# Four graph layers on one core: dealing out VectorE's side work anew, and normalising the last graph by halves

## The chip, the cores and the metric

The kernel runs on 1 core of one Trainium2 chip. The metric is the device time of one execution in microseconds. The kernel computes eight independent graphs, one after the other, in one launch. Its engines are TensorE (PE), VectorE (DVE), ScalarE (ACT), GpSimd (POOL) and SyncE (SP, which issues the plain loads, the transposing transfers and the stores).

## The reference

Input x is 8 x 1024 x 128 (float32), adj is 8 x 1024 x 1024 (0 or 1, about 16 ones in a row). Each graph passes four layers, and each layer adds its result to x and normalises the rows:

```
x = layernorm(x + relu([x, pool(x)] W + b))      # layer 0: pool = max over the first 25 neighbours
x = layernorm(x + elu(gat1(x, adj)))             # layer 1: softmax over neighbours, leaky relu scores
x = layernorm(x + elu(gat2(x, adj)))             # layer 2: the same form, other weights
x = layernorm(x + tanh(A tanh(A x W0 + b0) W1 + b1))   # layer 3: A = softmax(x Watt x' / sqrt(128) + mask)
layernorm(x) = (x - mean) / sqrt(var + 1e-5)     # over the 128 features
```

The maximum in layer 0 is taken over the neighbours with the 25 lowest indices of each node. It depends on the inputs alone, so a kernel may prepare it for a later graph.

## The kernel before, in words

The 1024 nodes of a graph lie in eight tiles of 128. While graph b passes its layers, the pooling of graph b+1 is prepared beside it, by two ways whose results are combined by a maximum.

**Gathered neighbours.** DVE finds a list of neighbour rows for two tiles at a time (a pair): `find_keys` (L1228 and its neighbours, "keys"), then `split_keys`, `sort_members` and `list_rows` ("members a", "b", "c"). POOL then gathers the rows from memory (`gather`, L551 to L571): 18 transfers for each of tiles 0 to 3 and 16 for each of tiles 4 to 7, each followed by a short memset. The gathered rows of a tile lie in one of three buffers (a ring, RING = 3), so tile t waits in `gather` for the pooling of tile t-3, and tile 4 for that of tile 1. DVE reduces a tile by `pool_tile` (L1327 and L1328, "pool"), and that waits until all its transfers have landed. Each engine works through its instructions in the order in which they are written, so whatever stands behind such a wait on DVE waits too.

**Picked neighbours.** The neighbours beyond the gathered ones are selected by products: for pick q, ACT or DVE makes a 0/1 matrix (`make_hot`: L632 and L635 on ACT, L1375 on DVE; MADE_BY says who makes which half), PE multiplies it with x (L903), and DVE folds the product into the running maximum (`max_pick`, L1385 and L1387). There are 16 picks for each graph after the first (26 for the first, done before graph 0 begins). PE writes pick q only when `max_pick` has read the pick before it from the same bank: pick 14 waits for `max_pick` 13 (`spare_maxed(b + 1, 13)`).

**Where side work stands.** The table SIDE names the places in DVE's program of graph b at which side work for graphs b+1 and b+2 is done; FIRST_WORK does the same for the picks ahead of graph 0. The table before has keys of (b+1, pair 1) at the head of layer 0, pooling of tile 4 behind the attention tiles ("steps"), of tile 6 between `make_hot` 12 and `max_pick` 12 ("last step"), and of tile 7 behind the last addition to x ("end").

**The end of a graph on the other engines.** PE computes the second attention product (L1150) in eight tiles, with pick 13 after the second and pick 14 after the sixth; then it packs the adjacency bits of a pair of graph b+2 (`feed`, L850), does pick 15, counts neighbours for graph b+2 (L878 to L883) and turns the next graph's x (L946). ACT converts adjacency tiles (L586), makes `hot` 14, applies tanh (L774), reads the packed bits (`take_fed`, L643), takes the counts (L613), normalises its half of the nodes (L669) and takes the turned x (L660, then L724). SP turns the packed bits by a transposing transfer for DVE's `find_keys`.

**The norm.** `layer_norm` aggregates the moments of eight tiles (L1398), computes the reciprocal root by ten small instructions on 128x8 (L1401 to L1418), and normalises tiles 0 to 3 itself (L1422); ACT normalises tiles 4 to 7 (L669) once the last of the ten is done. In the two gat layers of the last graph, which has no picks beside it, PE finishes the heads of nodes 0 to 511 first, and DVE adds each half as it comes (`take_heads`, `add_heads`).

Of the kernel before, what the change touches and what calls it, by code (L numbers as in the profile page):

```python
# [13 lines left out]
I32 = mybir.dt.int32  # L14
# [48 lines left out]
class Steps:  # L63
# [8 lines left out]
    def link(self, instruction):  # L72
# [30 lines left out]
              20: [("pool", 0, 5)],  # L103
              24: [("pool", 0, 6)],
# [3 lines left out]
SIDE = {"layer 0": [("keys", 1, 1)],  # L108
        "gat 1": [("members", 1, 1)],
# [8 lines left out]
        "steps": [("pool", 1, 4), ("keys", 2, 0), ("members", 2, 0), ("pool", 1, 5)],  # L118
        "last step": [("pool", 1, 6)],
        "end": [("pool", 1, 7)]}  # L120
# [44 lines left out]
def build_graph_layers(nc, x, adj, w0, b0, w1, b1, a1, w2, a2, watt, w3a, b3a, w3b, b3b, out):  # L165
# [13 lines left out]
    with ExitStack() as ctx:  # L179
# [398 lines left out]
        def _(act):  # L578
# [142 lines left out]
            def graph(b, slot, in_loop):  # L721
# [44 lines left out]
                feed(b, slot, 3, in_loop)  # L766
                if exists(b, 1, B, in_loop):
                    make_hot(b + 1, 14)
# [8 lines left out]
                take_fed(b, 3, in_loop)  # L777
# [49 lines left out]
        def _(pe):  # L827
# [208 lines left out]
            def graph(b, slot, in_loop):  # L1036
# [175 lines left out]
        def _(dve):  # L1212
# [181 lines left out]
            def layer_norm(slot):  # L1394

                settle()
                for t in range(T):
                    done(nc.vector.bn_aggr(moments[:, t, :], stats[:, t, :]))  # L1398
                settle()

                link(nc.vector.tensor_scalar(spread[:, :], moments[:, :, 1], EPS, None, ALU.add))  # L1401

                link(nc.vector.tensor_scalar(rstd[:, :].bitcast(I32), spread[:, :].bitcast(I32), -0.5, RSQRT_GUESS,
                                             ALU.mult, ALU.add))
                link(nc.vector.tensor_tensor(error[:, :], rstd[:, :], rstd[:, :], ALU.mult))
                link(nc.vector.scalar_tensor_tensor(out=error[:, :], in0=error[:, :], scalar=-0.5,
                                                    in1=spread[:, :], op0=ALU.mult, op1=ALU.mult))
                link(nc.vector.scalar_tensor_tensor(out=rstd[:, :], in0=error[:, :], scalar=1.5,
                                                    in1=rstd[:, :], op0=ALU.add, op1=ALU.mult))

                link(nc.vector.tensor_tensor(error[:, :], rstd[:, :], rstd[:, :], ALU.mult))
                link(nc.vector.scalar_tensor_tensor(out=error[:, :], in0=error[:, :], scalar=-THIRD,
                                                    in1=spread[:, :], op0=ALU.mult, op1=ALU.mult))
                link(nc.vector.scalar_tensor_tensor(out=error[:, :], in0=error[:, :], scalar=THIRD * 10 / 3,
                                                    in1=error[:, :], op0=ALU.add, op1=ALU.mult))
                link(nc.vector.scalar_tensor_tensor(out=rstd[:, :], in0=error[:, :], scalar=1.875,
                                                    in1=rstd[:, :], op0=ALU.add, op1=ALU.mult))
                norm_scale.raised_by(nc.vector.scalar_tensor_tensor(  # L1418
                    out=offset[:, :], in0=moments[:, :, 0], scalar=-1.0, in1=rstd[:, :],
                    op0=ALU.mult, op1=ALU.mult))  # L1420
# [3 lines left out]
                x_normed.raised_by(last)  # L1424

            def gat(b, slot, layer, in_loop):
# [70 lines left out]
                else:  # L1497
                    for h in range(2):
                        take_heads(h)
                        add_heads(h)  # L1500
                layer_norm(slot)

            def graph(b, slot, in_loop):
                flat = xs[slot][:, :, :].rearrange("p t c -> p (t c)")
                side_work(b, slot, "layer 0", in_loop)
# [6 lines left out]
                for h in range(2):  # L1512
# [51 lines left out]
                layer_norm(slot)  # L1564
# [82 lines left out]
```

How the kernel before makes its waits and increments, by code:

```python
            def load_adj(b, t, freed=None, count=None):  # L417
                source = adj_tiles[b, t]
                if freed is not None:
                    sp.wait_ge(freed.sem, count)
                    sp.sem_inc(loads_begun, 1)
                adj_loaded[t % 2].raised_by(sp.dma_start(adj_in[:, t % 2, :], source))
# [1 line left out]
            def turn(b, slot, t):  # L424
                sp.wait_ge(adj_converted.sem, adj_converted.at(b, t + 1))
                sp.sem_inc(loads_begun, 1)
                adj_t_ready[t % 2].raised_by(sp.dma_start_transpose(adj_t[slot][:, :, t * P:(t + 1) * P],
                                                                    adj_bf[:, t % 2, :]))
# [1 line left out]
            def turn_packed(b, pair):  # L430
                sp.wait_ge(packed_taken.sem, packed_taken.at(b, pair + 1))
                if not (isinstance(b, int) and b == 1 and pair == 0):
                    sp.sem_inc(loads_begun, 1)
                    sp.wait_ge(packed_read.sem, packed_read.at(b, pair))
                sp.sem_inc(loads_begun, 1)
                packed_turned.raised_by(sp.dma_start_transpose(
                    packed_t[:, :, :, :].rearrange("p h i g -> p (h i) g"),
                    group_bits[:, :, :].rearrange("p h n -> p (h n)")))
# [1 line left out]
            def load_next(b, t):  # L441
                if isinstance(b, int) and b == 0 and t < 4:
                    sp.wait_ge(first_read, 1)
                load_adj(b, t, adj_converted, adj_converted.at(b, t - 1))
```

## Time and profile before

| | |
|---|---|
| median of 3 runs | 1952.48 us (1941.37 to 1954.05) |
| the profiled execution, its time | 1933.09 us |
| its span in the profile | 1931.0 us |
| mean granted TensorE clock | 0.952 |
| PE busy | 1671.2 us (87%) |
| POOL busy | 1445.9 us (75%) |
| DVE busy | 1429.5 us (74%) |
| ACT busy | 1127.9 us (58%) |

All terms below come from the profiled execution. The span begins with the picks of graph 0 (to about 190 us), then graphs 0 to 6 follow in some 222 us each, and graph 7, which has nothing prepared beside it, takes the last 180 us. A row of a timeline gives the start, the duration, the engine, the line of the program and the operation; "xN" merges N like instructions that follow each other, and the bracket at its end gives the time that the engine sat idle before it, and who ended that.

### The profile page before, as it was taken

How to read it: one execution, taken by the hardware profiler on the slowest of the kernel's cores; microseconds unless marked ns; L12 is line 12 of the kernel's file. 1: busy time of each engine (PE TensorE's matmuls, PEld its weight loads, DVE VectorE, ACT ScalarE, POOL GpSimd, SP SyncE). 2: the span in 40 equal slices, each digit the busy share in tenths (PEclk: the TensorE clock that was granted, in tenths of full speed). 3: DMA queues.
4: the chain of work that ended last, by engine and by line, in shares of the span. 5: the costliest groups of instructions: out<-in, count | busy, mean ns of one | idle time of the engine just before them, and what ended most of it. 6: DMA issues, size and time to landing. Idle time of an engine off the chain costs nothing.

```text
span 1931.0 us, 29391 instructions
## 1 busy us (share of the span) xinstructions
PE 1671.2 (87%) x9767; PEld 1316.0 (68%) x9812; DVE 1429.5 (74%) x3427; ACT 1127.9 (58%) x1517; POOL 1445.9 (75%) x2135
## 2 busy tenths in 40 slices
PE   4777798999889898999989899998989898896777
PEld 2655676777759676677758677686757777595747
DVE  5874888768877789768886788768887688746531
ACT  6664755656665765656565665558556665652252
POOL 6888888888888888888788888888878887870000
PEclk9998899989999999998999999998999999997889
DMA  7231424343343333344233333435233522311010
GB/s 195 71 84 37 103 78 100 90 125 78 77 131 73 103 78 98 107 99 111 73 119 86 102 79 76 129 77 127 72 102 87 121 57 63 107 36 33 1 66 12
DMA packets 153282, 167.06 MB, mean 87 GB/s; under 512 B 102685, under 2 KB 119978, under 8 KB 153130
## 3 DMA queue, kind: packets, MB, share of 16 engines
q1 hardware_dynamic: 119594, 96.43, 18.6%
q0 software_dynamic: 33536, 68.75, 13.5%
q8 instruction: 77, 1.26, 0.3%
q14 instruction: 75, 0.61, 0.1%
HBM read 140.45 MB, written 4.19 MB: 75 GB/s over the span
## 4 chain that ended last, share of the span: by engine, by line
PE 43%; DVE 27%; ACT 9%; POOL 8%; issue 7%; DVEq 6%; DMA 1%; ACTq 0%; SPq 0%; POOLq 0%
PE spare L903 11%; PE big L1150 6%; POOL gathered L563 6%; PE big L1011 5%; DVEq L73 4%; PE big L1087 3%; PE big L935 3%; DVE probs_t L1454 3%; PE big L1109 3%; DVE pooled L1327 3%; ACT hot L632 2%; PE side L1127 2%; POOL pause L568 2%; DVE keys L1224 2%; PE big L1002 2%
## 5 line engine op out<-in xcount | busy, mean ns | idle before, releaser
L563 POOL DMA_INDIRECT gathered<-in_x_dram,rows x1048 | 1089.3, 1039 | 240.1 <-issue 158.4
L903 PE MATMUL spare<-hot,x_part 128*128 128x512 f32 x1552 | 393.4, 405 | 36.2 <-DVE hot L1375 27.3
L568 POOL MEMSET pause<- 32x256 bf16 x1048 | 349.9, 334 | 41.9
L903 PEld LDWEIGHTS spare<-hot,x_part 128*128 128x128 f32 x1552 | 291.4, 193 | 108.9 <-issue 21.2
L632 ACT ACTIVATE hot<-running,minus_count 128x2048 fp32r<-128x2048 bf16 (+1 forms) x131 | 251.1, 1916 | 131.8 <-PE spare L903 112.8
L635 ACT ACTIVATE hot<-hot,plus_one 128x2048 fp32r<-128x2048 f32 (+1 forms) x131 | 251.5, 1920 | 4.3
L1011 PEld LDWEIGHTS big<-values,probs_t 128*128 128x128 f32 x1792 | 219.8, 199 | 8.6
L1011 PE MATMUL big<-values,probs_t 128*128 128x129 f32 x1792 | 222.7, 283 | 0.4
L1327 DVE TENSOR_REDUCE pooled<-gathered 128x128 f32<-128x2048 f32 (+2 forms) x56 | 212.0, 3786 | 14.3 <-DMA gathered<-in_x_dram,rows 13.3
L1375 DVE TENSOR_SCALAR hot<-running 128x2048 fp32r<-128x2048 bf16 (+1 forms) x145 | 186.4, 1305 | 33.9 <-PE spare L903 16.4
L1454 DVE SCALAR_TENSOR_TENSOR probs_t<-side,col_gain,adj_t 128x1024 f32<-128x1024 f32 x128 | 154.6, 1276 | 27.3 <-ACT side L691 27.3
L1531 DVE TENSOR_REDUCE neg_max<-big 128x1 f32<-128x1024 f32 x64 | 78.1, 1220 | 98.8 <-PE big L1113 98.2
L903 PE MATMUL side<-hot,x_part 128*128 128x512 f32 x448 | 115.3, 402 | 28.8 <-DVE hot L1375 17.8
L613 ACT CAST running<-spare 128x512 bf16<-128x512 f32 x92 | 53.9, 586 | 140.4 <-remote 75.3
L745 ACT ACTIVATE work<-big,neg_max 128x1024 f32<-128x1024 f32 x64 | 71.4, 1116 | 98.8 <-DVE neg_max L1531 98.8
L1109 PE MATMUL big<-xt,queries 128*128 128x512 f32 x256 | 121.0, 595 | 6.5 <-ACT values L677 6.1
L1150 PEld LDWEIGHTS big<-values,probs_t 128*128 128x128 f32 x1024 | 117.6, 192 | 2.5 <-ACT values L677 0.9
L903 PEld LDWEIGHTS side<-hot,x_part 128*128 128x128 f32 x448 | 80.5, 188 | 56.0 <-issue 15.8
L1150 PE MATMUL big<-values,probs_t 128*128 128x128 f32 x1024 | 117.9, 274 | 0.7 <-ACT values L677 0.7
L1087 PE MATMUL big<-values,probs_t 128*128 128x128 f32 x1024 | 118.3, 274 | 0.0
L1087 PEld LDWEIGHTS big<-values,probs_t 128*128 128x128 f32 x1024 | 116.2, 192 | 0.0
L712 ACT ACTIVATE work<-work 128x512 f32<-128x512 f32 x32 | 20.0, 624 | 139.4 <-DVE work L1472 139.4
(203 smaller groups left out, 2629.5 us busy)
## 6 DMA issues: line engine op xcount, KB each, us to landing
adj_in<-in_adj_dram SPq DMA_DIRECT2D x128, 512.0 KB, 3.7
gathered<-in_x_dram,rows POOLq DMA_INDIRECT x1048
xs<-in_x_dram SPq DMA_DIRECT2D x8, 512.0 KB, 4.7
out_dram<-xs SPq DMA_DIRECT2D x8, 512.0 KB
adj_t<-adj_bf SPq DMA_TRANSPOSE x64
packed_t<-group_bits SPq DMA_TRANSPOSE x28, 2.8
w_sb<-in_L_gnn_W_dram SPq DMA_DIRECT2D x1, 128.0 KB
w_sb<-in_L_gnn_W_dram SPq DMA_DIRECT2D x2, 64.0 KB
```

What stands on the lines that cost most here:

```text
L563: (late_gathered if late else rows_gathered[t % RING]).raised_by(pool.indirect_dma_start(out=gathered[:, t % RING, k * C:(k + 1) * C], out ...
L568: last = nc.gpsimd.memset(pause[quarter:quarter + 32, k // (4 * PAUSED), :], 0.0)
L632: hot_apart.raised_by(nc.scalar.activation(chunk, running[:, tiles[0]:tiles[-1] + 1, :], ACT.Abs, bias=minus_count[:, s:s + 1]))
L635: hot_made.raised_by(nc.scalar.activation(chunk, chunk.bitcast(F32), ACT.Relu, scale=-1.0, bias=plus_one[:, 0:1]))
L903: last = nc.tensor.matmul(pick_bank(b, q), x_parts[part][:, m, :], hot[:, place_of(b, q, m), :], start=(m == 0 and part == 0), stop=(m == ...
L1011: last = nc.tensor.matmul(heads[:, t, 0:C + 1], probs_t[:, j, t * P:(t + 1) * P], values[:, j, :], start=False, stop=(j == T - 1), skip_gr ...
L1087: last = nc.tensor.matmul(low_t[:, t, :], probs_t[:, m, t * P:(t + 1) * P], values[:, m, 0:C], start=(m == 0), stop=(m == T - 1))
L1109: nc.tensor.matmul((low, high)[t % 2][:, half], queries[:, t * P:(t + 1) * P], xt[:, half], start=True, stop=False, skip_group_check=True)
L1150: last = nc.tensor.matmul(low_t[:, t, :], probs_t[:, m, t * P:(t + 1) * P], values[:, m, 0:C], start=(m == 0), stop=(m == T - 1))
L1327: link(nc.vector.tensor_reduce(pooled[:, t, :], rows_of[:, :, 0:n], AX.X, ALU.max))
L1375: hot_ready.raised_by(nc.vector.tensor_scalar(hot_chunk(b, q, c), running[:, tiles[0]:tiles[-1] + 1, :], float(wanted(b, q)), None, ALU.is ...
L1454: gat_probs.raised_by(nc.vector.scalar_tensor_tensor(out=probs_t[:, j, :], in0=gains, scalar=col_gain[:, j:j + 1], in1=adj_t[slot][:, j, : ...
```

## The change

In SIDE and FIRST_WORK, DVE's stages are moved. Keys of (graph b+2, pair 1) are now found near the end of graph b ("turned"), those of (1, 1) during the first graph's picks, and none at the head of layer 0. Tile 4 is pooled at attention tile 5, tile 6 in "steps" and tile 7 in "last step", which itself now stands behind `max_pick` 12 and `make_hot` 13 and ahead of `max_pick` 13. The last pick's maximum comes behind the norm. PE's packing for layer 3 moves from behind the attention product to behind its second tile, and ACT's reading of it ahead of `make_hot` 14. In the last graph, layers 0 to 2 call `layer_norm_half` for each half of the nodes as it is added, in place of one `layer_norm`.

```
@@ the tables
+              22: [("keys", 1, 1)],
...
-SIDE = {"layer 0": [("keys", 1, 1)],
-        "gat 1": [("members", 1, 1)],
+SIDE = {"gat 1": [("members", 1, 1)],
...
-        "steps": [("pool", 1, 4), ("keys", 2, 0), ("members", 2, 0), ("pool", 1, 5)],
-        "last step": [("pool", 1, 6)],
-        "end": [("pool", 1, 7)]}
+        "tile 5": [("pool", 1, 4)],
+        "steps": [("keys", 2, 0), ("members", 2, 0), ("pool", 1, 5), ("pool", 1, 6)],
+        "last step": [("pool", 1, 7)],
+        "turned": [("keys", 2, 1)]}
@@ ACT, layer 3
                 feed(b, slot, 3, in_loop)
+                take_fed(b, 3, in_loop)
                 if exists(b, 1, B, in_loop):
                     make_hot(b + 1, 14)
...
-                take_fed(b, 3, in_loop)
@@ PE, layer 3
+                    if t == 1 and exists(b, 2, B, in_loop):
+                        feed(b, slot, 3, in_loop)
                     if t in (1, 5) and exists(b, 1, B, in_loop):
...
-                    feed(b, slot, 3, in_loop)
@@ DVE, the norm
+            def layer_norm_half(slot, h):
+
+                scale_rows(slot, range(HALF * h, HALF * h + HALF))
+                if h == 0:
+                    norm_first_half(slot)
+                else:
+                    norm_scale.raised_by(offset_rows(slice(HALF, T)))
@@ DVE, a gat layer of the last graph
                         take_heads(h)
                         add_heads(h)
+                        layer_norm_half(slot, h)
+                    return
@@ DVE, layer 0
                     half_stats(slot, h)
+                    if not exists(b, 1, B, in_loop):
+                        layer_norm_half(slot, h)
@@ DVE, end of a graph
-                side_work(b, slot, "last step", in_loop)
                 if picks:
                     max_pick(b + 1, 12)
                     make_hot(b + 1, 13)
+                side_work(b, slot, "last step", in_loop)
+                if picks:
                     max_pick(b + 1, 13)
+                side_work(b, slot, "turned", in_loop)
                 for h in range(2):
                     dve.wait_ge(att_tanh.sem, att_tanh.at(b, 2 + h + 1))
...
-                side_work(b, slot, "end", in_loop)
+                layer_norm(slot)
                 if picks:
                     max_pick(b + 1, 15)
-                layer_norm(slot)
```

`scale_rows(slot, tiles)` holds the aggregation and nine of the ten small instructions, on the columns of the tiles named; `offset_rows` is the tenth, and `norm_first_half` normalises tiles 0 to 3.

## Rows read from the trace of the kernel before

**Rows 1.** The page, busy time of each engine, share of the span, instructions.

```profile
PE 1671.2 (87%) x9767; PEld 1316.0 (68%) x9812; DVE 1429.5 (74%) x3427; ACT 1127.9 (58%) x1517; POOL 1445.9 (75%) x2135
```

**Rows 2.** Who waited for whom: us in total, times, longest.

```profile
POOL gathered L563 <- DVE pooled L1328: 24.2, 5, 7.4
...
DVE pooled L1327 <- DMA gathered<-in_x_dram,rows: 13.3, 3, 7.5
```

**Rows 3.** Timeline of POOL: first gathers of tiles; one slow gather at 623.61.

```profile
408.16 0.95 POOL L563 DMA_INDIRECT gathered<-in_x_dram,rows  x1 [0.83 <-POOL pause L568]
...
623.61 1.75 POOL L563 DMA_INDIRECT gathered<-in_x_dram,rows  x1 [0.16 <-issue]
...
626.53 1.34 POOL L563 DMA_INDIRECT gathered<-in_x_dram,rows  x1 [0.83 <-POOL pause L568]
...
961.64 0.95 POOL L563 DMA_INDIRECT gathered<-in_x_dram,rows  x1 [6.26 <-DVE pooled L1328]
...
1065.98 0.95 POOL L563 DMA_INDIRECT gathered<-in_x_dram,rows  x1 [0.83 <-POOL pause L568]
```

**Rows 4.** Timeline of DVE, end of graph 1.

```profile
609.56 2.55 DVE L1375 TENSOR_SCALAR hot<-running 128x2048 fp32r<-128x2048 bf16 x2
...
622.24 0.69 DVE L1553 TENSOR_TENSOR xs<-xs,xt 128x512 f32<-128x512 f32 x1 [6.59 <-ACT xt L774]
...
632.05 3.71 DVE L1327 TENSOR_REDUCE pooled<-gathered 128x128 f32<-128x2048 f32 x1
...
636.27 0.69 DVE L1387 TENSOR_TENSOR best_t<-best_t,side 128x512 f32<-128x512 f32 x1
```

**Rows 5.** Timeline of DVE, keys at the head of graph 2 and what follows.

```profile
641.31 0.17 DVE L1241 TENSOR_SCALAR isolated<-degree 128x2 f32<-128x2 f32 x1
...
647.93 0.69 DVE L1508 TENSOR_TENSOR probs_t<-big,best_t 128x512 f32<-128x512 f32 x1 [0.42 <-PE big L1058]
```

**Rows 6.** Timeline of PE, end of graph 1: pick 14, first count, turning.

```profile
621.82 3.89 PE L903 MATMUL spare<-hot,x_part 128*128 128x512 f32 x16
...
633.86 0.38 PE L881 MATMUL side<-adj_t,count_all 128*128 128x512 bf16 x1
...
639.01 1.04 PE L946 MATMUL big<-ident,xs 128*128 128x128 f32 x8
```

**Rows 7.** Timeline of ACT, last count taken and start of graph 2.

```profile
639.21 0.59 ACT L613 CAST running<-side 128x512 bf16<-128x512 f32 x1
...
643.09 0.98 ACT L724 COPY work<-side 1x1024 f32<-1x1024 f32 x1
```

**Rows 8.** Timeline of ACT, the L724 copy of graphs 1, 6 and 7.

```profile
419.97 0.99 ACT L724 COPY work<-side 1x1024 f32<-1x1024 f32 x1
...
1529.07 0.98 ACT L724 COPY work<-side 1x1024 f32<-1x1024 f32 x1
...
1750.97 0.98 ACT L724 COPY work<-side 1x1024 f32<-1x1024 f32 x1
```

**Rows 9.** Timeline of DVE, pooling of tile 1 ends, graphs 1 and 6.

```profile
516.42 0.35 DVE L1328 TENSOR_SCALAR pooled<-pooled,connected,pool_floor 128x128 f32<-128x128 f32 x1
...
1625.42 0.35 DVE L1328 TENSOR_SCALAR pooled<-pooled,connected,pool_floor 128x128 f32<-128x128 f32 x1
```

**Rows 10.** Chain that ended last: last gather of graph 0's tile 7, issue to landing.

```profile
190.02 2.47 DMA gathered<-in_x_dram,rows
```

**Rows 11.** Timeline of DVE at graph 0's start, behind tile 7 and keys.

```profile
202.07 0.69 DVE L1508 TENSOR_TENSOR probs_t<-big,best_t 128x512 f32<-128x512 f32 x1
```

**Rows 12.** Timeline of DVE, last graph: norm of layer 0, second heads of layer 1.

```profile
1762.99 0.64 DVE L1398 BATCH_NORM_AGGREGATE moments<-stats 128x2 f32<-128x6 f32 x8
...
1765.89 0.17 DVE L1418 SCALAR_TENSOR_TENSOR offset<-moments,rstd 128x8 f32<-128x8 f32 x1
...
1799.76 0.18 DVE L1471 RECIPROCAL recip<-big 128x4 f32<-128x4 f32 x1 [3.11 <-PE big L1002]
```

**Rows 13.** Timeline of PE, last graph: turning after idle time.

```profile
1808.02 1.97 PE L946 MATMUL big<-ident,xs 128*128 128x128 f32 x8 [8.30 <-DVE xs L1422]
```

More of the change, by code:

```diff
@@ L1392, in half_stats, with scale_rows @@
                     done(nc.vector.bn_stats(stats[:, t, :], xs[slot][:, t, :]))
-            def layer_norm(slot):
+            def scale_rows(slot, tiles):
                 settle()
-                for t in range(T):
+                for t in tiles:
                     done(nc.vector.bn_aggr(moments[:, t, :], stats[:, t, :]))
                 settle()
[L1401 to L1420, printed above, removed]
@@ new lines, in scale_rows @@
+                part = slice(tiles[0], tiles[-1] + 1)
+                link(nc.vector.tensor_scalar(spread[:, part], moments[:, part, 1], EPS, None, ALU.add))
+                link(nc.vector.tensor_scalar(rstd[:, part].bitcast(I32), spread[:, part].bitcast(I32), -0.5,
+                                             RSQRT_GUESS, ALU.mult, ALU.add))
+                link(nc.vector.tensor_tensor(error[:, part], rstd[:, part], rstd[:, part], ALU.mult))
+                link(nc.vector.scalar_tensor_tensor(out=error[:, part], in0=error[:, part], scalar=-0.5,
+                                                    in1=spread[:, part], op0=ALU.mult, op1=ALU.mult))
@@ new lines, in scale_rows @@
+                link(nc.vector.scalar_tensor_tensor(out=rstd[:, part], in0=error[:, part], scalar=1.5,
+                                                    in1=rstd[:, part], op0=ALU.add, op1=ALU.mult))
+                link(nc.vector.tensor_tensor(error[:, part], rstd[:, part], rstd[:, part], ALU.mult))
+                link(nc.vector.scalar_tensor_tensor(out=error[:, part], in0=error[:, part], scalar=-THIRD,
+                                                    in1=spread[:, part], op0=ALU.mult, op1=ALU.mult))
@@ new lines, in scale_rows, with offset_rows @@
+                link(nc.vector.scalar_tensor_tensor(out=error[:, part], in0=error[:, part], scalar=THIRD * 10 / 3,
+                                                    in1=error[:, part], op0=ALU.add, op1=ALU.mult))
+                link(nc.vector.scalar_tensor_tensor(out=rstd[:, part], in0=error[:, part], scalar=1.875,
+                                                    in1=rstd[:, part], op0=ALU.add, op1=ALU.mult))
+            def offset_rows(part):
+                return nc.vector.scalar_tensor_tensor(
+                    out=offset[:, part], in0=moments[:, part, 0], scalar=-1.0, in1=rstd[:, part],
+                    op0=ALU.mult, op1=ALU.mult)
@@ L1421, in layer_norm, with norm_first_half @@
+            def norm_first_half(slot):
                 for t in range(T // 2):
@@ L1424, in layer_norm @@
                 x_normed.raised_by(last)
+            def layer_norm(slot):
+                scale_rows(slot, range(T))
+                norm_scale.raised_by(offset_rows(slice(0, T)))
+                norm_first_half(slot)
+            def layer_norm_half(slot, h):
+                scale_rows(slot, range(HALF * h, HALF * h + HALF))
+                if h == 0:
+                    norm_first_half(slot)
+                else:
+                    norm_scale.raised_by(offset_rows(slice(HALF, T)))
             def gat(b, slot, layer, in_loop):
@@ L1504, in graph @@
                 flat = xs[slot][:, :, :].rearrange("p t c -> p (t c)")
-                side_work(b, slot, "layer 0", in_loop)
                 for h in range(2):
@@ L1560, in graph @@
                             max_pick(b + 1, 14)
-                side_work(b, slot, "end", in_loop)
+                layer_norm(slot)
                 if picks:
                     max_pick(b + 1, 15)
-                layer_norm(slot)
             def pack_first():
```

## The prediction

> **What bounds the kernel now.** I read the page's busy times first: PE 1671 us and POOL 1446 us stand highest [rows 1], and neither is at its whole span, so the order of the work decides. The waits come next. DVE waited for gathered rows only three times in all, and POOL for DVE's pooling five times, 24.2 us [rows 2]. The reader should see two loops that run almost abreast: PE, DVE and ACT need (1529.07 - 419.97) / 5 = 221.8 us for a graph, by the L724 copy that I take as each graph's mark M [rows 8]; POOL needs less, since it is held up now and then. Third, POOL's tile boundaries. In graph 0 it starts the tile behind tile 7 at 408.16, in graph 1 at 626.53. In graph 3 it starts tile 4 at 961.64, released by DVE's pooling of tile 1, and is through tile 7 at 1065.98: 104.3 us for four tiles [rows 3]. A last gather landed 2.47 us after its start [rows 10]; the next tile's first gather starts some 2.1 us after it (0.95 gather, 0.3 memset, 0.83 idle), so a tile is in 0.3 us behind that start.
>
> Now DVE's side. Tile 7 is pooled at 632.05 without a wait [rows 4], 5 us after it landed (626.8). The change puts that pooling behind `make_hot` 13, which ends at 609.56 + 2.55 = 612.1. The data is not there for another 14.7 us. That is the heart of the matter.
>
> **The change, part by part.**
>
> *Tile 7.* Let L be the landing. Behind it, on DVE in order, stand: pooling 4.2 (632.05 to 636.27), `max_pick` 13, 0.7 [rows 4], so L + 4.9. Only then may PE start pick 14. Then keys, 641.31 to 647.5 = 6.2 [rows 5]: L + 11.1. Then the first half's addition and statistics, 1.6, begun at 622.24 when its tanh ended that idle time of 6.59 [rows 4] and now long ready: L + 12.8. `make_hot` 15, two chunks like the pair in [rows 4], 2.4 to 2.6: first chunk at 14.0, second at 15.3. PE meanwhile: pick 14, 3.9 [rows 6], two attention tiles 3.6, to L + 12.4. Pick 15 starts at 14.1 and ends at 18.0. From the first count to the turning is 5.15 [rows 6]; from it to ACT's last count copy 639.80 - 633.86 = 5.9 [rows 6, 7]: L + 24.0. ACT's four normalisations take 1.65 and the rest to the mark 1.14 (643.09 less the 641.95 at which its first copy of the turned x begins) [rows 7]. So the next M = L + 26.7. DVE's norm, done at L + 22, and `max_pick` 15 at L + 22.8 are hidden by ACT's counts, which is also why moving the norm ahead of `max_pick` 15 gains nothing here.
>
> *Where L falls.* POOL has been busy without a break up to 408.16, so nothing DVE does makes it earlier: L = 408.5 in graph 0, and M of graph 1 is 435.2 instead of 419.97, +15.2. From there each graph closes a loop. M to the end of pooling tile 1 is 96.8 in graph 1 and 96.7 in graph 6 (the first and last of six) [rows 8, 9]; this stretch is untouched. POOL starts tile 4 some 0.8 later, needs 104.3, landing 0.3: L = M + 202.2, while DVE stands at the pooling at 612.1 - 420.0 = M + 192.1, a wait of 10 us in every graph. The loop is 202.2 + 26.7 = 228.9, against 221.8: +7.1 a graph. After five more graphs M of graph 6 is 1579.7 (before 1529.07), +50.6. Its own end has no keys and no counts: L + 4.9 for `max_pick` 13, pick 14 and two attention tiles 7.5, tanh 1.1, addition 1.6, scale 3.1, ACT 2.8, together L + 21.0. So M of graph 7 is 1579.7 + 202.2 + 21.0 = 1802.9 against 1750.97 [rows 8], **+51.9**. The pooling does leave the end of graph 6, where it stood behind the last addition for 4.8 us, but the wait is what ends last.
>
> *Tiles 4 and 6.* They swap 4.2 us of DVE work around the same `max_pick` 11. Tile 6 lands 26 us before tile 7, at about M + 176, and is wanted at M + 177: no cost, or 1 to 2 us inside the later wait. In graph 0 it costs more, and that too only shortens the wait for 408.5.
>
> *Keys.* In graph 0 the first `pooled_t` stood behind keys at 202.07 [rows 11]; tile 7 was done 6 us before. Those 6.0 us are won and then waited away, because L of graph 0 is POOL's. In later graphs DVE is idle 0.42 behind the keys [rows 5]: nothing is won. In the first phase keys go before pooling of tile 6, which waited for its rows; at most 1 us, again behind a wait.
>
> *Packing.* On PE 1.0 us moves ahead of pick 13, behind the transposing transfers of two adjacency tiles. No row shows their landing; between 0 and 3 us of PE wait (the transfers are issued within 2 us of ACT's conversions). I take 1, by the nearest rows, the packed words' 2.8 us to landing; PE's coming stall for `max_pick` 13 covers it. ACT's `take_fed` waits for it ahead of `hot` 14, where ACT stood idle for pick 13 anyway. SP's transfer of the packed bits then comes some 18 us earlier, and SP's next wait is for the output, unchanged.
>
> *The last graph by halves.* One norm takes 1762.99 to 1766.06 up to the offset, 3.1, and 4.1 with DVE's own tiles [rows 12]. Half the columns save only the four aggregations (0.3); the small instructions cost the same on four columns as on eight, as far as the rows go (a bound from below: half, which would save 1 us more). So the first half costs 3.5 and delays the second half's addition, already ready in layer 0, and the scale then comes 3.2 later. Since PE can turn half of x ahead, I take +3.1 for layer 0. In the gat layers the idle 3.11 before the second heads [rows 12] covers 3.1 of 3.5; the turning behind the norm has four transposes left, -0.2 each. Sum **+2.7**, bounds 0 and +5.
>
> Sum: 1933.1 + 51.9 + 2.7 = 1987.7 on the profiled execution's scale, +54.6. The median of the runs is 1952.5, 19.4 above that execution; the difference carried over gives **2007 us**, +2.8%.
>
> **The rivals.** *A, PE falls to its low clock in the stalls.* After 8.30 us idle, eight transposes took 1.97, at 1.2 GHz, against 1.04 at 2.4 GHz [rows 13, 6]. PE now idles 5 to 7 us before pick 14. In my sum the slower pick 14 and attention hide behind keys and `make_hot` 15 up to 1.7 us; if the clock costs 3.9 more, 2.2 to 3.6 us stay, times six: 2020 to 2029. The Trainium skill, "TensorE: Matmul & The Clock Gate", "What's actually happening", says an idle array falls to half rate; by that rule this rival holds, and the trace agrees on the fall.
>
> *B, the gathers get faster.* Beside a `make_hot` of DVE a gather took 1.75 instead of 0.95 [rows 3]. If moved work avoided all of them, 64 gathers at 1.455 and four boundaries of 0.7 more are 96 us instead of 104.3, L = M + 193.9, the loop 220.6, below 221.8; only graph 0's shift and the halves stay, 1952.5 + 15.2 + 2.7 = 1970 on the median's scale, within 1%. Against it: the number of `hot` made per graph is unchanged. The Trainium skill, "GPSIMD Engine Reference", "Key points", has GpSimd share its SBUF interfaces with VectorE; by it the collisions move with the instructions, they don't vanish.
>
> *C, the other side: keys were on the path of every graph.* If tile 7 lands by M + 192 and each graph's head is bound by keys as in graph 0, 6.2 us go seven times, 5.5 at graph 6's end, and +2.7 remains: -46, 1906. It decides from L below 612 in graph 1; L is 626.8 [rows 3], and the idle 0.42 [rows 5] speaks against it too.
>
> *D, no wait but heads as I read them*: -6 - 5.5 - 3 + 2.7 = -12, 1941: within 1%.
>
> **How the numbers follow.** A measurement here tells about 1% from no change. Forecast 0.78, A 0.10, B 0.06, D 0.03, C 0.03. Slower 0.88, same 0.09, faster 0.03. The range takes the runs' spread (1941 to 1954) with 5 to 8.5 us a graph: 1941 + 15 + 25 + 0 = 1981, and 1954 + 15 + 50 + 5 = 2024; a little towards B makes 1976, towards A 2026.
>
> **What would show it.** DVE idle before L1327 or its like for DMA gathered, 9 to 12 us in each of graphs 1 to 6 and over 15 in graph 0; L724 copies 228 to 230 apart; POOL waiting for L1328 some 11 us a graph before tile 4; pick 14 released by `max_pick`; the last graph 2 to 3 us longer from its mark. It is wrong if `pool_tile` of tile 7 starts unwaited, or if L724 copies stay 222 apart.

## The result, and the profile after

| | before | after |
|---|---|---|
| median | 1951.01 us (1941.37 to 1954.05, 4 runs) | 1988.70 us (1978.24 to 1993.82, 4 runs) |
| profiled execution, its time | 1933.09 us | 1988.97 us |

The ratio is 1.0199, with a 95% interval of [1.0156, 1.0241]: slower, by 37.7 us. The forecast was 2007 (1976 to 2026). On the scale of the profiled executions the forecast was 1987.7, and it came out at 1988.97. The 18 us between the two forecasts are taken up behind the experiments.

The span is 1987.2 us, 56.2 more than before, and no engine's busy time has grown by as much: PE's is 28.6 us above [rows 1], that of its weight loads 12.7, and the others' differ by 7 us or less.

```profile
PE 1699.8 (86%) x9812; PEld 1328.7 (67%) x9812; DVE 1436.3 (72%) x3454; ACT 1127.0 (57%) x1517; POOL 1448.0 (73%) x2135
```

The waits after (us in total, times, longest) answer [rows 2]: both have grown. DVE waits for gathered rows 80.2 us instead of 13.3, POOL for pooling 73.5 instead of 24.2. A new wait of ACT, ahead of its copy at L753, was ended by nothing that the trace can name ("remote"); such waits are called ownerless below.

```profile
DVE pooled L1329 <- DMA gathered<-in_x_dram,rows: 80.2, 11, 12.6
...
POOL gathered L564 <- DVE pooled L1330: 73.5, 7, 13.5
...
ACT probs_t L753 <- remote: 26.8, 4, 7.8
```

The timeline of DVE after, at tile 7 in graphs 0 and 1, answers the row at 632.05 of [rows 4], which had no wait. `max_pick` 13 stands behind it.

```profile
407.24 3.58 DVE L1329 TENSOR_REDUCE pooled<-gathered 128x128 f32<-128x2048 f32 x1 [12.63 <-DMA gathered<-in_x_dram,rows]
...
636.44 3.79 DVE L1329 TENSOR_REDUCE pooled<-gathered 128x128 f32<-128x2048 f32 x1 [6.97 <-DMA gathered<-in_x_dram,rows]
640.31 0.35 DVE L1330 TENSOR_SCALAR pooled<-pooled,connected,pool_floor 128x128 f32<-128x128 f32 x1
640.75 0.69 DVE L1389 TENSOR_TENSOR best_t<-best_t,spare 128x512 f32<-128x512 f32 x1
```

The timeline of POOL after, at the gather behind tile 7 of graph 1 and at the first gather of tile 4 in graph 2, answers [rows 3]: the wait before tile 4 is 10.75 us. In graphs 1 to 6 it is 10.6 to 13.6 us, where before it was 0.8 to 7.4 (6.26 in the row of graph 3).

```profile
635.84 0.95 POOL L564 DMA_INDIRECT gathered<-in_x_dram,rows  x1 [0.83 <-POOL pause L569]
...
759.82 0.95 POOL L564 DMA_INDIRECT gathered<-in_x_dram,rows  x1 [10.75 <-DVE pooled L1330]
```

The marks after (ACT's copy, now at L725) answer [rows 8].

```profile
433.95 0.98 ACT L725 COPY work<-side 1x1024 f32<-1x1024 f32 x1
...
1581.74 0.98 ACT L725 COPY work<-side 1x1024 f32<-1x1024 f32 x1
...
1804.13 1.00 ACT L725 COPY work<-side 1x1024 f32<-1x1024 f32 x1 [0.95 <-PE side L1048]
```

A graph takes (1581.74 - 433.95) / 5 = 229.6 us. In graph 1, tile 7 landed at 636.2, M + 202.2. The page's shares of the chain that ended last, by engine, show the same turn: POOL had 8% of it before, and has 20% now.

```profile
PE 33%; POOL 20%; DVE 17%; issue 14%; ACT 10%; DVEq 3%; DMA 2%; another core or an unknown queue 1%; SPq 0%; POOLq 0%; ACTq 0%
```

PE's timeline at the end of graph 1, to be held against [rows 6], shows a delay that the forecast had made too small. The packing (L851) waits for the transposing transfer, and pick 13 stands behind it. Pick 14 comes at 643.91 without idle time before it, although `max_pick` 13 had waited for tile 7: that was done at 640.75 + 0.69 = 641.44. PE's own path was 2.5 us later than DVE's.

```profile
626.11 3.73 PE L1151 MATMUL big<-values,probs_t 128*128 128x128 f32 x32
632.32 1.03 PE L851 MATMUL packed<-adj_t,pack_w 128*128 128x256 bf16 x8 [2.47 <-DMA adj_t<-adj_bf]
633.11 3.90 PE L904 MATMUL spare<-hot,x_part 128*128 128x512 f32 x16
...
643.91 3.89 PE L904 MATMUL spare<-hot,x_part 128*128 128x512 f32 x16
```

The same two times can be read in every graph. In graphs 0, 3 and 6 pick 14 starts within 0.1 us of the end of `max_pick` 13, so the wait for tile 7 holds it. In graphs 1, 2, 4 and 5 it starts 2.5, 3.2, 1.2 and 4.4 us later, held by PE's own work. So two delays run side by side. The experiments are there to part them.

### The profile page after: what moved, and what is told of

It is laid out like the page before. It is cut to its first block, busy times and chain, and to the rows that moved or that the text cites. A ratio compares the mean times of both kernels' runs of the same rounds, so it can differ in the third digit from the quotient of the medians.

```text
span 1987.2 us, 29496 instructions
## 1 busy us (share of the span) xinstructions
PE 1699.8 (86%) x9812; PEld 1328.7 (67%) x9812; DVE 1436.3 (72%) x3454; ACT 1127.0 (57%) x1517; POOL 1448.0 (73%) x2135
## 4 chain that ended last, share of the span: by engine, by line
PE 33%; POOL 20%; DVE 17%; issue 14%; ACT 10%; DVEq 3%; DMA 2%; another core or an unknown queue 1%; SPq 0%; POOLq 0%; ACTq 0%
POOL gathered L564 15%; PE spare L904 7%; PE big L1012 5%; POOL pause L569 5%; PE big L1151 3%; PE big L936 3%; PE big L1088 2%; ACT hot L633 2%; DVE probs_t L1475 2%; PE big L1110 2%; DVE hot L1377 2%; DVEq L73 2%; DVE pooled L1329 2%; PE side L904 1%; ACT xs L670 1%
## 5 line engine op out<-in xcount | busy, mean ns | idle before, releaser
L904 PE MATMUL spare<-hot,x_part 128*128 128x512 f32 x1552 | 404.8, 414 | 56.2 <-DVE hot L1377 22.0
L904 PEld LDWEIGHTS spare<-hot,x_part 128*128 128x128 f32 x1552 | 299.9, 199 | 133.0 <-issue 28.9
L569 POOL MEMSET pause<- 32x256 bf16 x1048 | 357.0, 341 | 42.2
L1329 DVE TENSOR_REDUCE pooled<-gathered 128x128 f32<-128x2048 f32 (+2 forms) x56 | 212.5, 3794 | 81.2 <-DMA gathered<-in_x_dram,rows 80.2
L1012 PEld LDWEIGHTS big<-values,probs_t 128*128 128x128 f32 x1792 | 226.8, 204 | 10.1 <-issue 1.3
L1012 PE MATMUL big<-values,probs_t 128*128 128x129 f32 x1792 | 230.5, 289 | 0.7 <-issue 0.5
L1475 DVE SCALAR_TENSOR_TENSOR probs_t<-side,col_gain,adj_t 128x1024 f32<-128x1024 f32 x128 | 154.6, 1276 | 27.2 <-ACT side L692 25.6
L1088 PE MATMUL big<-values,probs_t 128*128 128x128 f32 x1024 | 124.1, 276 | 3.3 <-issue 2.5
L1088 PEld LDWEIGHTS big<-values,probs_t 128*128 128x128 f32 x1024 | 118.6, 191 | 6.7 <-issue 6.5
L1151 PEld LDWEIGHTS big<-values,probs_t 128*128 128x128 f32 x1024 | 117.6, 192 | 2.5 <-ACT values L678 0.9
L1151 PE MATMUL big<-values,probs_t 128*128 128x128 f32 x1024 | 117.9, 274 | 0.7 <-ACT values L678 0.7
L753 ACT COPY probs_t<-side 128x1024 f32<-128x1024 f32 x64 | 64.3, 1004 | 69.3 <-PE side L1128 39.8
```

The lines of the kernel that those rows point to most:

```text
L569: last = nc.gpsimd.memset(pause[quarter:quarter + 32, k // (4 * PAUSED), :], 0.0)
L904: last = nc.tensor.matmul(pick_bank(b, q), x_parts[part][:, m, :], hot[:, place_of(b, q, m), :], start=(m == 0 and part == 0), stop=(m == ...
L1012: last = nc.tensor.matmul(heads[:, t, 0:C + 1], probs_t[:, j, t * P:(t + 1) * P], values[:, j, :], start=False, stop=(j == T - 1), skip_gr ...
L1329: link(nc.vector.tensor_reduce(pooled[:, t, :], rows_of[:, :, 0:n], AX.X, ALU.max))
L1475: gat_probs.raised_by(nc.vector.scalar_tensor_tensor(out=probs_t[:, j, :], in0=gains, scalar=col_gain[:, j:j + 1], in1=adj_t[slot][:, j, : ...
```

## The experiments

They ran in three groups. Beside them the kernel before had medians of 1965.2, 1960.0 and 1933.4 us (1951.0 beside the result); each ratio is against the runs of its own group, and medians of different groups are not to be subtracted. The first and third group ran on a chip with the number 11, the second on one with the number 13; that of the result isn't known. So the 32 us between the first and the third group don't go with the chip's number. Per graph, the profiled executions are compared by the mean distance of the marks of graphs 1 to 6 (five graphs), which was 221.8 us before and is 229.6 after.

**Tile 7 alone.** The kernel before, with the pooling of tile 7 moved and nothing else.

```
-        "end": [("pool", 1, 7)]}
+        "before 13": [("pool", 1, 7)]}
...
+                side_work(b, slot, "before 13", in_loop)
+                if picks:
                     max_pick(b + 1, 13)
...
-                side_work(b, slot, "end", in_loop)
```

> The kernel before with one edit: tile 7 is pooled ahead of max_pick 13 instead of behind the last addition to x. Keys, packing, tiles 4 and 6, the norm and the last graph stay as before. Theory (the wait for tile 7's rows closes a loop through GpSimd): DVE waits 9 to 15 us for gathered rows in each of graphs 0 to 6, L724 copies lie 222 to 226 apart (the loop is 202.2 us to the landing and 21 to 25 us behind it, since no keys stand in the tail), the span grows by 15 to 40 us. Rival 1 (the moved keys and the packing make the loss): span within 5 us of before. Rival 2 (the wait is hidden by PE's own work): DVE waits, but the L724 copies stay 222 apart and the span grows by under 8 us.

Measured: 1985.01 us, 19.8 more than its group's 1965.18, ratio 1.0103 [1.0065, 1.0141]; the marks of graphs 1 and 7 lie at 435.39 and 1810.27, 229.1 apart on the mean (230.5 in the five graphs up to graph 6's mark). DVE's timeline at tile 7 of graph 1, PE's at the pick 14 behind it, and the stretch of that pick (us, busy of PE, PEld, DVE, ACT, POOL, granted TensorE clock, DMA share, GB/s):

```profile
636.57 3.58 DVE L1327 TENSOR_REDUCE pooled<-gathered 128x128 f32<-128x2048 f32 x1 [12.23 <-DMA gathered<-in_x_dram,rows]
```

```profile
641.41 5.57 PE L903 MATMUL spare<-hot,x_part 128*128 128x512 f32 x16 [6.53 <-DVE best_t L1387]
```

```profile
641.40:647.00 5.60, 5.59 (x18) 4.49 (x19) 2.66 (x6) 0.00 (x0) 5.07 (x6) 0.69 0.14 35
```

This one edit by itself makes a wait of 8.8 to 12.2 us in each of graphs 0 to 5, and a loop as long as that of the kernel after. My theory had the marks 222 to 226 apart, and that was too little. The part behind the landing took 27.8 to 29.5 us and not 21 to 25. Pick 14 can start some 5 us behind the landing, and from there to the next mark it is 21.0 to 21.4 us in graphs 1 to 5 of the kernel before, which makes 26 already. Here it is 22.7 to 23.3: PE had sat idle for 3.4 to 6.5 us before pick 14, which then took 5.6 to 6.6 us instead of 3.9, in graph 1 at a granted clock of 0.69. That is what rival A described.

**The kernel after without it.** Everything else of the change stays.

```
-        "last step": [("pool", 1, 7)],
+        "end": [("pool", 1, 7)],
...
                     max_pick(b + 1, 15)
+                side_work(b, slot, "end", in_loop)
```

> The changed kernel with one edit: tile 7 is pooled behind the last pick's maximum at the very end of the graph, all else as changed. Theory (the wait for tile 7): DVE no longer waits for tile 7 except up to 3 us in graph 0, L725 copies lie 220 to 223 apart, the span falls by 45 to 62 us, to 1925 to 1942. Rival 1 (keys near the graph's end and the packing ahead of pick 13 cost): copies stay over 226 apart. Rival 2 (the engines are held up by something ahead of pick 13, and the wait only hides it): copies 225 to 228 apart, the span falls by 10 to 30 us.

Measured: 1989.4 us, ratio 1.0108 [1.0051, 1.0165]. My theory fell, and rival 1 held. The wait for tile 7 is gone, and graphs 1 to 5 still take (1591.53 - 431.30) / 5 = 232.0 us. Only graph 6, which packs nothing, became shorter: 216.0 us from its mark to the next instead of 222.4. PE's timeline at the end of graph 4 shows a part of the loss: the packing waits, and the pick behind it takes 5.46 us instead of 3.9. Another part are ownerless waits ahead of ACT's L753, 49.7 us in seven times.

```profile
1319.90 3.73 PE L1151 MATMUL big<-values,probs_t 128*128 128x128 f32 x32
1326.13 1.17 PE L851 MATMUL packed<-adj_t,pack_w 128*128 128x256 bf16 x8 [2.50 <-DMA adj_t<-adj_bf]
1326.95 5.46 PE L904 MATMUL spare<-hot,x_part 128*128 128x512 f32 x16
```

**Packing alone.** The kernel before with the feed moved (third group).

```
+                    if t == 1 and exists(b, 2, B, in_loop):
+                        feed(b, slot, 3, in_loop)
...
-                    feed(b, slot, 3, in_loop)
                     pick(b + 1, 15)
@@ ACT
                 feed(b, slot, 3, in_loop)
+                take_fed(b, 3, in_loop)
```

> The kernel before with one part of the change alone: PE packs layer 3's adjacency behind the second attention tile, and ACT reads it ahead of hot 14. Theory: the packing waits for the transposing transfer, and PE's next products stand behind it with no long DVE wait to cover them, so pick 13 comes 3 to 5 us later in each of graphs 0 to 5. From the first to the third tanh of the attention heads it is 31 to 33 us instead of 27.2, and the ratio is 1.009 to 1.017. Rival, as the prediction had it (1 us, covered): distance under 29 us, ratio 0.998 to 1.004.

Measured: 1959.95 us against 1933.42, ratio 1.0143 [1.0127, 1.0158]: +26.5 us. ACT applies the tanh in four groups, two for the first product of the attention (L759) and two for the second (L774); from the first to the third group it is 30.7 to 34.2 us in graphs 0 to 5, where it was 27.2. The theory held in the ratio, and the distances spread a little wider than its 31 to 33. PE's timeline at the end of graph 1, then a table by stretch (us, busy of PE, PEld, DVE, ACT, POOL, granted TensorE clock, DMA share, GB/s):

```profile
617.39 1.86 PE L850 MATMUL packed<-adj_t,pack_w 128*128 128x256 bf16 x8 [3.49 <-DMA adj_t<-adj_bf]
618.91 5.76 PE L903 MATMUL spare<-hot,x_part 128*128 128x512 f32 x16
624.50 7.30 PE L1150 MATMUL big<-values,probs_t 128*128 128x128 f32 x64
```

```profile
603.00:611.00 8.00, 8.00 (x49) 6.55 (x49) 7.75 (x7) 3.88 (x8) 7.20 (x9) 1.00 0.30 67
617.00:624.50 7.50, 7.11 (x24) 5.52 (x25) 0.00 (x0) 2.32 (x2) 5.83 (x11) 0.61 0.37 113
625.00:631.00 6.00, 6.00 (x56) 6.00 (x56) 0.39 (x1) 5.97 (x5) 5.20 (x9) 1.00 0.17 48
```

The attention product before it ended at 613.90. Three terms follow: 3.5 us of wait (2.4 to 3.5 in the six graphs), 1.5 us from the packing's start to the pick's, and a pick of 5.76 us instead of 3.9. Behind the idle time the granted clock is 0.61 on the mean of the stretch, part of it at 1.2 GHz and the rest at 2.4; before and after it is 1.00. The second transpose was issued from 610.39 to 611.62; its data released PE 5.8 us later.

**Tile 1 earlier** (second group), to give POOL its start back: as tile 7 alone, with tile 1 pooled in the first gat layer's heads.

```
-        "gat 1 heads": [("keys", 1, 2), ("pool", 1, 0)],
+        "gat 1 heads": [("keys", 1, 2), ("pool", 1, 0), ("pool", 1, 1)],
-        "gat 2 heads": [("pool", 1, 1), ("keys", 1, 3)],
+        "gat 2 heads": [("keys", 1, 3)],
```

> As e1_pool7_alone (only tile 7's pooling moved ahead of max_pick 13), with tile 1 pooled in gat 1's place for tile 0 instead of in gat 2, so that GpSimd may start tile 4 some 10 us earlier in a graph. Theory (a loop: pooling tile 1, four gathered tiles, pooling tile 7, the rest of the graph): GpSimd no longer waits for pooling before tile 4, tile 7's rows land at 191 to 194 us behind the L724 copy, DVE waits under 4 us for them, and the copies lie as far apart as in the kernel before on this chip (222 to 226), against 229.1 in e1; the span falls by 15 to 25 us below e1's. Rival (the position of the pooling on DVE costs by itself, by its 4.2 us ahead of max_pick 13): copies stay at 227 or more.

Measured: 2010.99 us, ratio 1.0270 [1.0226, 1.0314]. A miss: it is worse than tile 7 alone, and graphs 1 to 5 take 234.8 us. POOL did start tile 4 at M + 86 without a wait, as I wanted. Its timeline in graph 1, at the first gather of tile 5:

```profile
562.67 0.95 POOL L563 DMA_INDIRECT gathered<-in_x_dram,rows  x1 [17.17 <-DVE pooled L1328]
```

The loop closes one tile later: tile 5 waits for the pooling of tile 2, which had not moved, and tile 7 is again waited for 11.2 us. Besides, 4 us of pooling now lie in the first gat layer's heads, and from the norm of layer 0 to the norm of that layer it is 3.1 to 5.6 us longer than in the profiled kernel before. So the rival, that the place on DVE costs by itself, held in part, for tile 1.

**Keys and packing back** (second group). As the kernel after without tile 7's move, with keys at the head of layer 0 and the feed where they were. What stays are tiles 4 and 6, the norm ahead of the last maximum with tile 7 last, and the halves.

```
-                    if t == 1 and exists(b, 2, B, in_loop):
-                        feed(b, slot, 3, in_loop)
...
+                    feed(b, slot, 3, in_loop)
                     pick(b + 1, 15)
...
-              22: [("keys", 1, 1)],
...
+SIDE = {"layer 0": [("keys", 1, 1)],
```

> As e2_pool7_last (the changed kernel with tile 7 pooled last), with keys of pair 1 back at the head of layer 0 and TensorE's packing and ScalarE's reading of it back behind the attention product. What stays of the change: tiles 4 and 6 dealt anew, the norm ahead of the last maximum, the halves. Theory now (the packing ahead of pick 13 waits for the second transposing transfer, which lands 5.9 us after its issue, and costs 3.5 to 5 us a graph by itself): copies 222 to 226 apart instead of e2's 229.4, span 15 to 30 us below e2's. Rival (dealing out tiles 4 and 6 costs): copies stay over 227 apart.

Measured: 1974.64 us, ratio 1.0089 [1.0054, 1.0125]. From the first to the third group of tanh it is 27.2 us again, so what the packing had added to that stretch went with it; the ratio can't show it, since its interval overlaps that of the kernel with the packing, 1.0108. Graphs 1 to 5 take 228.0 us, more than the 222 to 226 of my theory. 0.9% is left, and the stretch that has grown is the one before it: from `max_pick` 10 to the first tanh 15.8 to 19.7 us, where the profiled kernel before has 14.0 in all seven graphs. The trace puts it down to ownerless waits of ACT:

```profile
ACT probs_t L752 <- remote: 50.8, 8, 7.8
```

**Tiles 4 and 6 alone**, to see whether that re-deal brings such waits about (third group).

```
-        "steps": [("pool", 1, 4), ("keys", 2, 0), ("members", 2, 0), ("pool", 1, 5)],
-        "last step": [("pool", 1, 6)],
+        "tile 5": [("pool", 1, 4)],
+        "steps": [("keys", 2, 0), ("members", 2, 0), ("pool", 1, 5), ("pool", 1, 6)],
+        "last step": [],
```

> The kernel before with one part of the change alone: tile 4 is pooled at attention tile 5, and tile 6 ahead of the eleventh maximum; tile 7 stays behind the last addition. Theory: nothing waits for these moves by a semaphore, but with tile 4 gone from the head of this stage, keys and members run beside PE's second stage of the attention; ACT's and PE's ownerless idle times between the tenth maximum and the first tanh grow from 14 to 16 us to 16 to 20 us, 1 to 3 us a graph, ratio 1.004 to 1.010. Rival, as the prediction had it (no cost): ratio 0.997 to 1.003, the distance as in the kernel before.

Measured: 1937.20 us, ratio 1.0024 [1.0015, 1.0034], and 14.0 us in all seven graphs. My theory fell: the re-deal doesn't bring ownerless waits about by itself. Whether it lengthens them where they occur isn't shown, since no kernel of this group has any ahead of L752. The cost lies in graph 0, whose period is 235.2 us instead of 227.4, because tile 6 is pooled ahead of `max_pick` 11 before it has landed. DVE's timeline there:

```profile
377.80 3.67 DVE L1328 TENSOR_REDUCE pooled<-gathered 128x128 f32<-128x2048 f32 x1 [5.20 <-DMA gathered<-in_x_dram,rows]
381.55 0.38 DVE L1329 TENSOR_SCALAR pooled<-pooled,connected,pool_floor 128x128 f32<-128x128 f32 x1
382.02 0.69 DVE L1388 TENSOR_TENSOR best_t<-best_t,spare 128x512 f32<-128x512 f32 x1
```

The following graphs take 221.4 on the mean (before 221.8).

**The kernel before again**, unchanged, one execution in the first group.

> The kernel before, unchanged, for its trace: its profiled execution took 1933 us, the median of its runs 1951. Theory (the engines are held up for some us at places where no semaphore holds them, in some graphs of some executions): an execution near 1950 us has graph periods of two kinds, near 222 and 4 to 6 us above, and the longer ones have idle time on ACT or PE ended by no engine, between the third last and the last copy of the attention weights. Rival (the gathers are slower in such an execution): the distance between the first gathers of tiles 4 and of the next tile 0 grows from 104 to over 106 us and DVE waits for rows.

Measured: 1958.37 us. The same code has here what its first profile lacked: ACT stands 31.2 us in five ownerless waits ahead of L752. PE's timeline in graph 2, and ACT's beside it:

```profile
817.36 1.04 PE L1127 MATMUL side<-ident,work 128*128 128x128 f32 x8
818.23 4.08 PE L1087 MATMUL big<-values,probs_t 128*128 128x128 f32 x31
822.56 1.18 PE L1087 MATMUL big<-values,probs_t 128*128 128x128 f32 x5 [0.25 <-issue]
823.99 3.66 PE L1087 MATMUL big<-values,probs_t 128*128 128x128 f32 x28 [0.26 <-issue]
```

```profile
814.46 1.01 ACT L752 COPY probs_t<-side 128x1024 f32<-128x1024 f32 x1 [3.15 <-PE side L1127]
822.54 1.01 ACT L752 COPY probs_t<-side 128x1024 f32<-128x1024 f32 x1 [7.07 <-remote]
```

PE had written what ACT copies (L1127, to 818.40) 4.1 us before the copy started, and PE itself paused twice; after the first pause it goes on at 822.56, when ACT's copy starts too. From `max_pick` 10 to the first tanh it is 14.0 to 18.1 us, and that stretch holds 15.4 of the 25.3 us by which this span exceeds the first profile's. The rest lies elsewhere, 7.0 us of it between the norms of the two gat layers. Five of the periods came out as the theory said (225.1 to 227.9 us, one of 221.3), and POOL's gathers were not slower. So a part of the difference between 1933 and the medians of 1951 to 1965 us are such waits, and the profiled execution of before, at 1933.09, was one without them in this stage.

**The halves alone**, one execution in the first group.

```
+                    if not exists(b, 1, B, in_loop):
+                        layer_norm_half(slot, h)
...
+                        layer_norm_half(slot, h)
+                    return
```

> The kernel before with the last graph's norms by halves in layers 0 to 2, and nothing moved elsewhere. Theory: from the L724 copy of graph 7 to the end 3.0 us more than the 180.0 of before: layer 0 is 3 to 4 us longer, the two gat layers within 0.5 us each. Rival (halving helps every layer, since PE turns the first half earlier): 2 to 6 us less than 180.0.

Measured: 1951.55 us. The last graph takes 180.37 us from its mark, which against the 180.03 of before looks like nothing. DVE's timeline tells more. The last `offset` of layer 0:

```profile
1787.87 0.16 DVE L1421 SCALAR_TENSOR_TENSOR offset<-moments,rstd 128x4 f32<-128x4 f32 x1
```

That is 18.4 us behind the mark (1769.43), where [rows 12] has 1765.89 - 1750.97 = 14.9: +3.5 in layer 0, as expected. After the second gat layer it is 96.8, against 96.0 in the profiled before and 93.4 and 93.7 in two other executions without halves. The last graph's length from its mark spreads by itself: 178.3 to 182.1 us in the eight profiled executions without halves, 180.4 to 184.5 in the five with halves in three layers, and 180.1 with halves in the gat layers alone (below). The two means, 179.5 and 182.4, differ by 2.9 us, and all of it that can be located is in layer 0.

**The tail after the norm** (second group). The kernel before with the part of the change that seemed sound: keys of (1, 1) among graph 0's picks, halves in the gat layers alone, and the end of a graph in this order.

```
-                side_work(b, slot, "last step", in_loop)
...
                     max_pick(b + 1, 13)
+                side_work(b, slot, "last step", in_loop)
...
-                side_work(b, slot, "end", in_loop)
+                layer_norm(slot)
                 if picks:
                     max_pick(b + 1, 15)
-                layer_norm(slot)
+                side_work(b, slot, "end", in_loop)
```

> The kernel before with: keys of graph 1's pair 1 in the first phase, tile 6 pooled between max_pick 13 and the first addition (where DVE sat idle 6.6 us), tile 7 behind the norm and the last maximum, and the halves in the two gat layers of the last graph alone. Theory: no wait for rows but up to 2 us in graph 0; 5 to 6 us less up to graph 1's copy, 5 us less at the end of graph 6, 0.5 us less in each graph between, the last graph within 0.5 us of before: 10 to 16 us faster, ratio 0.992 to 0.995. Rival (the head of a graph, where tile 7's pooling and keys now stand in a row ahead of the turned pooling, becomes DVE-bound): copies 1 to 3 us further apart and no gain.

Measured: 1938.85 us against 1960.04, ratio **0.9907** [0.9875, 0.9939]: faster than the kernel before, and in the same group the kernel after had 1990.6. To part it, two more ran in the third group, both without halves. First the tail with graph 0's keys:

> The kernel before with two edits: tile 6 pooled between the thirteenth maximum and the first addition, and behind the last addition first the norm, then the fifteenth maximum, then tile 7; besides, keys of (1, 1) among graph 0's picks and not at the head of graph 0. No halves in the last graph. Theory that DVE's end of a graph was on the path: ratio 0.986 to 0.993, as the same kernel with halves had 0.991, and the last graph 1 us shorter by its mark than with halves. Rival (only graph 0's keys gained, 6.0 us): 0.996 to 0.998.

Measured: 1923.02 us, 0.9955 [0.9941, 0.9968]. Then the tail by itself:

> As the kernel with tail and first keys, but keys of (1, 1) stay at the head of graph 0. Theory (the end of a graph was on the path, some 1.5 to 3 us in each of seven graphs): ratio 0.989 to 0.996, 0.003 above the kernel with both. Rival (it was the keys): 0.999 to 1.001.

Measured: 1926.11 us, 0.9965 [0.9953, 0.9977]. The tail alone gives 7.3 us of 1933.4. Graph 0's keys give 3.1 more by the medians, which the runs don't set clear of noise (1922.73 to 1927.58 us with them, 1923.05 to 1930.09 without). For the two together I had expected 0.7 to 1.4%, for the tail 0.4 to 1.1%; it is 0.45% and 0.35%. Why the same edits, with halves in the gat layers besides, gave 21 us in the second group, where ownerless waits occur, was not tried apart. That the added slack takes some of them in is an argument, not shown.

**The kernel after again** (second group).

> The changed kernel, unchanged, beside the others on one chip. On the chip of e1 to e4, the wait alone cost 1.0103 and the moves without the wait 1.0108. Theory (the two costs lie on parallel paths, so the longer one counts): ratio 1.010 to 1.014, copies 228 to 230 apart. Rival (they add up): ratio 1.019 to 1.024, copies 231 or more apart.

Measured: 1990.6 us, 1.0163 [1.0127, 1.0198], and graphs 1 to 5 take 231.1 us. That lies between the ranges of the theory and of the rival, so the medians don't decide whether the costs hide each other. The profiled execution took 1998.46 us, 9.5 more than that of the result, with ACT's ownerless waits ahead of L753 at 46.1 us in seven times, 19.3 more. In it pick 14 starts 3.0 to 4.9 us behind `max_pick` 13 in graphs 1 to 5: there PE's path ended last in all five, and the wait for tile 7 in none.

## Why the prediction was right, and where it was not

**Where L falls: right.** L = M + 202.2 was forecast, and the six graphs that follow graph 0 give 200.5 to 203.0. The marks of graphs 1, 6 and 7 were forecast at 435.2, 1579.7 and 1802.9, and came at 433.95, 1581.74 and 1804.13. From L to the next mark 26.7 was forecast, and it is 26.7 to 29.3 in graphs 1 to 5. Tile 7 alone shows that this edit brings such a loop about by itself, ratio 1.0103. Rivals B, C and D are out: 12.2 us of wait in graph 1 of that kernel, and a period of 229.1.

**That this path alone ends last: only in part.** In graphs 0, 3 and 4 L + 26.7 holds to 0.2 us. In graphs 1, 2 and 5 it is 27.5, 28.3 and 29.3, since PE reached pick 14 by its own path 2.5, 3.2 and 4.4 us after `max_pick` 13 had freed it. Without the wait for tile 7 graphs 1 to 5 were no shorter, 232.0 us. So the wait is a sufficient cause of the longer graph and not a necessary one, and its price alone was 19.8 us of the median, not the 51.9 of the forecast. That 1987.7 met 1988.97 so closely is in part luck: the packing and the ownerless waits, which the sum hardly held, lay mostly beside the wait and not behind it, and the profiled execution of before was a fast one.

**The signs: some missed.** DVE's wait for tile 7 was to be over 15 us in graph 0 and 9 to 12 in graphs 1 to 6. It is 12.6 in graph 0 (7.0 more stood ahead of tile 6) and 7.0, 7.7, 11.1, 9.8 and 6.9 in graphs 1 to 5. L was in its place, so DVE came later, behind the longer stretches on PE and ACT. Pick 14 was to be released by `max_pick`; that holds in graphs 0, 3 and 6. The distance of the marks, 229.6, and POOL's waits of 10.6 to 13.6 us before tile 4 came as forecast.

**Packing: mis-sized, and the cover was misread.** I took 1 us, between 0 and 3, "PE's coming stall for `max_pick` 13 covers it". Alone it costs 26.5 us, or (1554.04 - 424.33) / 5 = 225.9 - 221.8 = 4.1 a graph in graphs 1 to 5. The nearest rows that I used, the packed words' landing, were the wrong kin: the transposing transfer of a tile lands 5.8 us after its issue. Two further terms were missing. At its old place the packing had waited for nothing (629.12 in graph 1, right behind the product), and the idle time before it brings the granted clock down, which is rival A's mechanism at another place. That it hardly shows in the sum has one reason: in the kernel after, this delay and the wait for tile 7 lie side by side, and both end before pick 14. Where the wait for tile 7 is taken away, the packing has to be paid: it is a part of the 1.0108 of the kernel after without tile 7's move.

**Rival A: its mechanism is real.** Pick 14 at 643.91, in graph 1 of the kernel after, had no idle time before it and took 3.89 us, at full speed. In all of graphs 1 to 5 it took 3.9, with at most 1.3 us of idle time before it. But in graph 0 PE sat idle for 5.49 us before it, and it took 6.05 us. With tile 7 alone this happens in every graph (5.5 to 6.6 us). In the kernel after the slow pick of graphs 2, 4 and 5 is pick 13, behind the packing, with 5.5 us each; in graphs 1 and 3 it took 3.90. The price that I put on it, another 13 to 22 us, did not come: the sum held.

**Tiles 4 and 6: right for the loop.** No cost is seen there. Alone they cost 7.9 us in graph 0, which I had put into the wait for 408.5; that held, since graph 1's mark came at 433.95, no later than forecast.

**Keys: right.** Nothing is won in the kernel after. Where nothing waits behind them, graph 0's keys give 3.1 us of the 6.0, within the noise.

**The last graph: right within its own spread.** 183.07 - 180.03 = +3.0 against +2.7. Layer 0 alone is +3.1 (18.0 against 14.9).

**From the profiled execution to the median: wrong.** I added 19.4 us to both sides. In the runs beside the result the median of before lies 17.9 us above its profiled execution, and that of after 0.3 below its own. The first had no ownerless waits ahead of L752, the second had 26.8 us of them ahead of L753. So the offset stood for something that the profile of before lacked and that of after holds. Up to L the kernel after takes such waits in, where it has 7 to 13 us of waiting in each of graphs 0 to 5, which POOL sets: M to L is 200.5 to 203.0 whether it is 15.4 or 19.6 us from `max_pick` 10 to the first tanh. Behind L it doesn't take them in wholly, as the graphs of PE's path show, and its second profiled execution, with 19.3 us more of them, took 9.5 longer. The difference of the profiled pair is 55.9 us; of the medians, 37.7. Without the offset the forecast was 1987.7, against a median of 1988.7; that it fits so well is luck again.

## What to carry to other kernels

A consumer moved ahead of its data costs the data's arrival plus everything that stands behind it on its queue. Where the producer's ring depends on that queue too, it is paid in every round of the loop, and here moving one release earlier only handed the wait to the next tile. Size each part of a change alone as well as in the sum: here two parts cost 1.0% and 1.4% alone and 1.6 to 2.0% with all the rest. The traces show them side by side, and the part of tile 7, taken back, won nothing in graphs 1 to 5. To know which of two delays ends last, compare in each graph when either frees the instruction that waits for both, and not in one graph alone. If the profiled execution is the fastest ever seen of its kernel, ask what the others wait for before carrying their distance over to a changed kernel.

## What the runs showed of the hardware

- ACT and PE lose 4 to 8 us at a time in the dense attention product (L1087), with operands ready and no semaphore named: 31.2 us in five times in one execution of the kernel before, none at L752 in its first profile, and none in any of the four kernels profiled in the third group, whose 15 runs of the kernel before lie within 1931.49 to 1935.34. The chip's number is the same, 11, in the first group, where they occur (1954.52 to 1974.96 in 10 runs). The cause stays open.
- A transposing transfer of 128x1024 (bf16) released PE 5.8 us after the end of its issue.
- Behind 3.49 us of idle time the granted TensorE clock was 0.61 over the next 7.5 us, and a pick took 5.76 instead of 3.9 us; behind 6.53 us it was 0.69 over 5.6 us, and a pick took 5.57. 8.30 us of idle time in [rows 13] had had the same kind of effect. Behind 2.5 us of it the pick took 3.90 in one graph and 5.46 or 5.48 in others.
